# An adapter chain and a mixture of low-rank experts on one core: the helper products and the load order of the prologue rewritten

## The chip, the cores and the metric

The kernel runs on 1 core of one Trainium2 chip. Times are microseconds (us) of one execution on the device. The engines are TensorE (PE), VectorE (DVE), ScalarE (ACT), GpSimd (POOL) and SyncE (SP); SP and ACT issue the DMA transfers.

## The reference

x is 8 samples of 512 tokens with 2048 features, in float32. Two residual layers follow each other. The first adds a rank-16 adapter that is picked per sample; the second adds a dense product with W and two gated experts of rank 16 out of eight.

```
Bx = einsum('bni,bri->bnr', x, B0[adapter_ids]);  x = x + einsum('bnr,bor->bno', Bx, A0[adapter_ids])
base   = einsum('btd,od->bto', x, W)                       # W: 2048 x 2048
logits = einsum('btd,ed->bte', x, Wr) + 5 * one_hot(language_ids)[:, None]
gates  = softmax of the two largest logits, at their places, 0 elsewhere
h      = einsum('btd,erd->bter', x, A)
x      = x + base + 2 * einsum('bter,bte,eor->bto', h, gates, B)
```

## The kernel before

**Numbers.** Every float32 factor is split into a high part in fp32r (ScalarE casts it) and a low part (VectorE subtracts), and a product is made of three matmuls: high by high, low by high, high by low.

**Stages.** The first sample is handled apart, in 36 slots; each slot takes one 128-row strip of one quarter of W's columns, transposes it on PE (`w_transpose`, L637), copies it back (`w_keep`, ACT), forms four sums of it for the later samples (`w_sums`, DVE), writes these to DRAM (`w_store`, `w_sums_store`, SP), splits it (`pair_hi`, ACT; `pair_lo`, DVE) and multiplies (`first_products`, 24 matmuls of 512 columns). The other seven samples reread the prepared strips from DRAM.

**The prologue**, in `pe_start`, `act_start`, `dve_start`, `pool_start` and `sp_start` (L1081 to L1251), is what the change rewrites. It makes, for sample 0:

- `awb`, the helper columns: 16 blocks of 128 features, each with the 128 columns of the expert matrices A (`an`), the 8 router columns Wr (`wrn`) and the 16 adapter columns B0 of the current sample, as high and low part. A and Wr are transposed two blocks at a time into banks 0 and 1 of PSUM (`small_transpose`, L920), eight times in turn; the B0 rows of all eight samples (`b0n`) are transposed in four groups (`b0_transpose`, L942), and the columns of sample 0 are copied out of them.
- x of sample 0, transposed: 16 units u of two blocks by 256 tokens. A load m brings two units. A unit is transposed (`x_transpose`), copied out of PSUM by ACT (`x_keep`, L318), split into `xah` and `xal` (two places each, so unit u waits for the products of unit u-2), and multiplied with `awb` (`aux_products`, L351; 8 matmuls). Units 0 to 7 and 8 to 15 are two halves, both summed in banks 4 and 5, so the second half waits until the first has been copied out (`aux_low`, `aux_sum`).
- `a0t`, the adapter's output matrices A0 of all samples, reordered by POOL (`a0p`), transposed twice (`a0_transpose`, eight groups) and split, by rows (`a0_rows_hi`, `a0_rows_lo`) and by blocks; `g_products` (L1018, 32 matmuls) multiplies them with `awb`.
- The adapter itself: `bx_transpose`, `delta` (PE), `adapt` (DVE), then `first_hi` and `first_lo` split the new x for the slots.

**Order.** Each engine runs its own list as written; semaphores join them. In `pe_start` all helper columns come before the units of x; then twelve steps s each transpose unit 4+s, multiply unit s and transpose one group of A0. SP's list before the slots is: helper matrices, B0 rows, A0, the store of the split B0 (`b0_scr`), W strips 0 and 1, then, once both halves of `a0_rows_lo` are there (semaphore c_ar): three rows of `a0g`, the two stores of `a_scr`, W strip 2, the stores of strip 0, W strip 3, the stores of strip 1, and Bm (`bn`, placed in `ost`). ACT issues the eight loads of x. POOL reorders `bn` into `bnj` (placed in `xst`), and PE transposes `bnj` at the start of slot 1 (`bt_transpose(0)`, L1042):

```
for i in range(SLOTS0):            # pe_main
    ...
    if i in (1, 2):
        bt_transpose(e, 2 * i - 2)
```

Two more waits are used below. `w_keep(2, 0)` waits until the store of strip 0 has landed (semaphore d_bs0), because strip 2 goes into the same place; and PE transposes the second half of strip 2 only after that copy.

Of the kernel before, what the change touches and what calls it, by code (L numbers as in the profile page):

```python
# [5 lines left out]
def adapted_moe_lora_kernel(nc, x, adapter_ids, language_ids, A0, B0, W, Wr, A, Bm, out):  # L6
# [4 lines left out]
    P = 128  # L11
# [8 lines left out]
    AW = NAUX + R  # L20
    LOW = 256
# [67 lines left out]
    with ctx:  # L89
# [86 lines left out]
        def four(b, q, half):  # L176
# [3 lines left out]
        c_pool, c_lang, c_ap, c_aph, c_apl, c_bp, c_bph, c_bpl, c_bb = (  # L180
            sem(n) for n in ("c_pool", "c_lang", "c_ap", "c_aph", "c_apl", "c_bp", "c_bph", "c_bpl", "c_bb"))
# [3 lines left out]
        d_ids, d_lid, d_a, d_b0, d_a0, d_bn = (sem(n) for n in ("d_ids", "d_lid", "d_a", "d_b0", "d_a0", "d_bn"))  # L185
# [8 lines left out]
        d_u3 = [sem(f"d_u3{c}") for c in range(2)]  # L194
        c_tr, c_xc, c_xh, c_xl, c_ax = (sem(n) for n in ("c_tr", "c_xc", "c_xh", "c_xl", "c_ax"))
# [95 lines left out]

        def x_transpose(e, n, u):
# [24 lines left out]

        def x_keep(e, n, u):  # L318
            q, kp = x_unit(u)
            if kp == 0 and n >= 1:  # L320
                b = n - 1
                if n == 1:
                    e.wait_ge(c_l0, 16)
                elif q < 2:
                    if n == 2:
                        wait_used(e, SLOTS0 - 1)
                    else:
                        e.wait_ge(c_spl, split_of(b - 1, 6, 3) + 1)
                else:
                    e.wait_ge(c_spl, split_of(b, q, 3) + 1)  # L330
                    e.wait_ge(c_add, 8 * b)
            e.wait_ge(c_tr, 16 * n + u + 1)
            e.copy(two(n, q, kp), pb[:, x_bank(n, u), :]).then_inc(c_xc, 1)

        def x_hi(e, n, u):
# [6 lines left out]
            e.copy(xah[:, u % 2, :, :].rearrange("p k t -> p (k t)"), two(n, q, kp)).then_inc(c_xh, 1)  # L342

        def x_lo(e, n, u):
            q, kp = x_unit(u)
            e.wait_ge(c_xh, 16 * n + u + 1)
            e.tensor_tensor(out=xal[:, u % 2, :, :].rearrange("p k t -> p (k t)"), in0=two(n, q, kp),  # L347
                            in1=xah[:, u % 2, :, :].rearrange("p k t -> p (k t)").bitcast(f32), op=ALU.subtract)\
             .then_inc(c_xl, 1)

        def aux_products(e, n, u):  # L351
            q, kp = x_unit(u)
            if u % 8 == 0:
                if n == 0 and u == 0:
                    e.wait_ge(c_bb, 2)
                elif n and u == 0:
                    e.wait_ge(c_gd, GD * (n - 1) + 5)
                    e.wait_ge(d_bc, 16 * n)
                else:
                    e.wait_ge(c_gd, GD * n + 1)  # L360
            e.wait_ge(c_xl, 16 * n + u + 1)
# [1207 lines left out]
```

## Time and profile before

| | us |
|---|---|
| three timed runs | 1622.21, 1624.8, 1625.4 (median 1624.8) |
| the profiled execution | 1623.4 |
| its span, first to last instruction | 1621.6 |
| its first product with W starts at | 76.96 |
| its slot 1 starts at | 85.67 |

In the rows further down, the idle time in brackets is that of the engine just ahead of the instruction, with what ended it. The span's first 77 us are the prologue; from there PE is almost always busy, and a stage is read from the stretch it lies in, not from the whole.

### The profile page before, as it was taken

How to read it: one execution, taken by the hardware profiler on the slowest of the kernel's cores; microseconds unless marked ns; L12 is line 12 of the kernel's file. 1: busy time of each engine (PE TensorE's matmuls, PEld its weight loads, DVE VectorE, ACT ScalarE, POOL GpSimd, SP SyncE). 2: the span in 40 equal slices, each digit the busy share in tenths (PEclk: the TensorE clock that was granted, in tenths of full speed). 3: DMA queues.
4: the chain of work that ended last, by engine and by line, in shares of the span. 5: the costliest groups of instructions: out<-in, count | busy, mean ns of one | idle time of the engine just before them, and what ended most of it. 6: DMA issues, size and time to landing. Idle time of an engine off the chain costs nothing.

```text
span 1621.6 us, 21156 instructions
## 1 busy us (share of the span) xinstructions
PE 1587.1 (98%) x7744; PEld 1336.5 (82%) x7744; DVE 1176.2 (73%) x1599; ACT 758.7 (47%) x1000; POOL 9.8 (1%) x19
## 2 busy tenths in 40 slices
PE   7799999999999999999999999999999999999998
PEld 5687888788888888888888888888888888888887
DVE  3575444687778976888768876888769877787665
ACT  4553344344544554455444554445544544445443
POOL 1000000000000000000000000000000000000000
PEclk9899999999999999999999999999999999999999
DMA  8689797879886887879977797878877788576665
GB/s 240 190 214 252 211 241 188 214 220 239 204 220 220 220 218 197 233 224 230 219 200 230 217 232 191 234 223 224 214 200 233 222 227 205 195 234 207 207 217 161
DMA packets 396985, 351.30 MB, mean 217 GB/s; under 512 B 250522, under 2 KB 323530, under 8 KB 395850
## 3 DMA queue, kind: packets, MB, share of 16 engines
q1 hardware_dynamic: 394706, 345.76, 77.5%
q10 hardware_dynamic: 2176, 4.19, 0.9%
q8 instruction: 61, 1.00, 0.3%
q14 instruction: 42, 0.34, 0.1%
HBM read 280.62 MB, written 68.82 MB: 215 GB/s over the span
## 4 chain that ended last, share of the span: by engine, by line
PE 93%; DMA 2%; ACT 1%; SPq 1%; DVE 1%; issue 1%; ACTq 0%; DVEq 0%
PE pb L746 27%; PE pb L747 27%; PE pb L748 27%; PE pb L366 4%; PE pb L368 3%; PE pb L514 2%; PE pb L649 1%; SPq L625 1%; PE pb L314 1%; DMA raw<-in_L_cond_W_dram 1%; DMA wrn<-in_L_cond_Wr_dram 1%; ACT xah L342 0%; DMA t_scr<-raw 0%; DMA t_scr<-tst 0%; DMA bt_scr<-bt 0%
## 5 line engine op out<-in xcount | busy, mean ns | idle before, releaser
L742 DVE TENSOR_TENSOR wl<-raw,wh 128x1024 fp32r<-128x1024 f32 (+1 forms) x456 | 555.1, 1217 | 333.9 <-ACT wh L738 333.7
L738 ACT CAST wh<-raw 128x1024 fp32r<-128x1024 f32 (+1 forms) x456 | 477.1, 1046 | 683.7 <-PE pb L748 675.6
L746 PE MATMUL pb<-wh,sh 128*128 128x512 f32 x1568 | 612.8, 391 | 0.5 <-DVE ost L782 0.5
L747 PE MATMUL pb<-wl,sh 128*128 128x512 f32 x1568 | 611.6, 390 | 0.0
L748 PE MATMUL pb<-wh,sl 128*128 128x512 f32 x1568 | 611.2, 390 | 0.0
L748 PEld LDWEIGHTS pb<-wh,sl 128*128 128x128 f32 x1568 | 294.3, 188 | 62.8
L746 PEld LDWEIGHTS pb<-wh,sh 128*128 128x128 f32 x1568 | 294.6, 188 | 56.2 <-DVE wl L742 0.9
L747 PEld LDWEIGHTS pb<-wl,sh 128*128 128x128 f32 x1568 | 294.6, 188 | 55.0
L366 PE MATMUL pb<-awb,xah 128*128 128x304 f32 x512 | 138.4, 304 | 2.9 <-DVE aux L381 1.6
L368 PE MATMUL pb<-awb,xal 128*128 128x256 f32 x512 | 134.4, 280 | 0.0
L746 PE MATMUL pb<-wh,xh 128*128 128x512 f32 x256 | 106.2, 415 | 1.2 <-DVE ost L782 0.8
L366 PEld LDWEIGHTS pb<-awb,xah 128*128 128x128 f32 x512 | 96.1, 188 | 7.7 <-DVE aux L381 1.8
L748 PE MATMUL pb<-wh,xl 128*128 128x512 f32 x256 | 102.0, 399 | 0.0
L747 PE MATMUL pb<-wl,xh 128*128 128x512 f32 x256 | 101.9, 398 | 0.0
L368 PEld LDWEIGHTS pb<-awb,xal 128*128 128x128 f32 x512 | 96.3, 188 | 4.2
L588 DVE TENSOR_TENSOR sl<-pool_a,sh 128x512 fp32r<-128x512 f32 x120 | 82.0, 684 | 0.0
L347 DVE TENSOR_TENSOR xal<-pool_a,xah 128x512 fp32r<-128x512 f32 x88 | 60.3, 686 | 18.8 <-ACT xah L342 18.7
L583 ACT CAST sh<-pool_a 128x512 fp32r<-128x512 f32 x120 | 73.5, 613 | 0.0
L660 ACT COPY raw<-pb 128x512 f32<-128x512 f32 x64 | 37.7, 589 | 68.2 <-PE pb L649 58.9
L521 DVE TENSOR_TENSOR pool_a<-pool_a,pb 128x512 f32<-128x512 f32 x88 | 58.8, 680 | 11.9 <-PE pb L514 11.9
L342 ACT CAST xah<-pool_a 128x512 fp32r<-128x512 f32 x88 | 54.7, 623 | 25.2 <-DVE pool_a L262 13.8
L748 PEld LDWEIGHTS pb<-wh,xl 128*128 128x128 f32 x256 | 49.0, 192 | 10.9
(135 smaller groups left out, 1280.6 us busy)
## 6 DMA issues: line engine op xcount, KB each, us to landing
raw<-t_scr SPq DMA_DIRECT2D x392, 512.0 KB, 4.4
xst<-in_x_dram SPq DMA_DIRECT2D x768, 32.0 KB, 3.7
raw<-in_L_cond_W_dram SPq DMA_DIRECT2D x128, 128.0 KB, 3.9
t_scr<-tst SPq DMA_DIRECT2D x32, 512.0 KB, 5.1
raw<-bt_scr SPq DMA_DIRECT2D x28, 512.0 KB, 3.9
out_dram<-ost SPq DMA_DIRECT2D x28, 512.0 KB, 4.4
out_dram<-u SPq DMA_DIRECT2D x28, 512.0 KB, 3.4
t_scr<-raw SPq DMA_DIRECT2D x32, 256.0 KB, 4.1
```

The source lines that it names most:

```text
L342: e.copy(xah[:, u % 2, :, :].rearrange("p k t -> p (k t)"), two(n, q, kp)).then_inc(c_xh, 1)
L347: e.tensor_tensor(out=xal[:, u % 2, :, :].rearrange("p k t -> p (k t)"), in0=two(n, q, kp), in1=xah[:, u % 2, :, :].rearrange("p k t -> p ...
L366: e.matmul(pb[:, 4 + t, 0:2 * AW], xah[:, u % 2, k, toks], cols[:, 0:2 * AW], start=u % 8 == 0 and k == 0, stop=False)
L368: last = e.matmul(pb[:, 4 + t, 0:LOW], xal[:, u % 2, k, toks], cols[:, 0:LOW], start=False, stop=u % 8 == 7 and k == 1)
L521: e.tensor_tensor(out=two(n, q, kp), in0=two(n, q, kp), in1=pb[:, delta_bank(n, u), :], op=ALU.add)\
L583: e.copy(sh[:, h % SR, :, :].rearrange("p k t -> p (k t)"), two(b, SUM_QUARTER[product], kp)).then_inc(c_sph, 1)
L588: e.tensor_tensor(out=sl[:, h % SR, :, :].rearrange("p k t -> p (k t)"), in0=two(b, SUM_QUARTER[product], kp), in1=sh[:, h % SR, :, :].rea ...
L738: e.copy(pair_split(wh, g), pair_source(g)).then_inc(c_wh, 1)
L742: e.tensor_tensor(out=pair_split(wl, g), in0=pair_source(g), in1=pair_split(wh, g).bitcast(f32), op=ALU.subtract).then_inc(c_wl, 1)
L746: e.matmul(o, h, wh[:, g % RING, k, :], start=start, stop=False)
L747: e.matmul(o, h, wl[:, g % RING, k, :], start=False, stop=False)
L748: return e.matmul(o, l, wh[:, g % RING, k, :], start=False, stop=stop)
```

## The change

- A is transposed in four groups of four blocks (`a_transpose`), each filling one of the banks 0 to 3; Wr and the B0 rows of sample 0 alone, loaded into rows 8 to 23 of `wrn`, are transposed as 16 pieces of 24 columns into bank 5 (`small_transpose`). Five copies and five subtractions take the place of eight and eight, and of the two copies of B0 columns.
- The transposes of all eight samples' B0 move from before the first units to steps 3 to 6, those of A0 from steps 3 to 10 to steps 7 to 14; the 32 `g_products` move behind step 15, in three parts between the steps of the adapter.
- Odd units of x are copied out of PSUM by DVE (`x_keep_dve`), even ones by ACT. `xah0` and `xal0` give two more places, so unit u waits for the products of unit u-4. The second half of the sums goes to banks 2 and 3.
- 18 transposes of `ident` (`warm`) stand ahead of everything on PE.
- SP issues seven of the eight loads of x, ahead of and between B0, A0 and W; W strips 0 and 1 are issued ahead of the store of B0.
- In the slots, `w_transpose(2, 1)` moves into slot 0, (3, 1) to the start of slot 1, and so on for the first two slots, and `first_hi` waits piece by piece for the memory that it overwrites. The split places share memory with the prologue's, so five of these are put in another order.

PE, from the first transposes to the first helper product. Before (`an`, `wrn`, `b0n` are A, Wr and B0 as loaded, `xst` and `ost` hold x):

```order
L314 MATMUL pb<-ident,xst 128x128 [waits d_x00,c_pool]
...
L927 MATMUL pb<-ident,an 128x128 [waits d_a]
L928 MATMUL pb<-ident,wrn 128x8
...
L927 MATMUL pb<-ident,an 128x128 [waits c_apl]
...
L948 MATMUL pb<-ident,b0n 128x128 [waits d_b0]
L948 MATMUL pb<-ident,b0n 128x128 x7
L948 MATMUL pb<-ident,b0n 128x128 [waits c_bpl]
...
L314 MATMUL pb<-ident,xst 128x128 [waits c_xc,d_x01]
...
L366 MATMUL pb<-awb,xah 128x304 [waits c_xl,c_bb]
```

And after:

```order
L957 MATMUL pb<-ident 128x128 [waits c_pool]
L957 MATMUL pb<-ident 128x128 x17
L321 MATMUL pb<-ident,xst 128x128 [waits d_x00]
...
L963 MATMUL pb<-ident,an 128x128 [waits d_a]
L963 MATMUL pb<-ident,an 128x128 x7
L969 MATMUL pb<-ident,wrn 128x24 [waits d_wr]
L969 MATMUL pb<-ident,wrn 128x24 x15
L963 MATMUL pb<-ident,an 128x128 x8
L321 MATMUL pb<-ident,xst 128x128 [waits c_x00,d_x01]
...
L388 MATMUL pb<-awb,xah 128x304 [waits c_xl,c_apl]
```

The waits of the transposes on the subtractions (c_apl) and the B0 transposes are gone from this place.

SP, from A0 to the stores that follow it. Before:

```order
L1223 DMA a0n<-in_L_cond_A_dram 128x256 [waits c_tr]
L1223 DMA a0n<-in_L_cond_A_dram 128x256 x7
L1227 DMA b_scr<-b0h 2048x1x128 [waits c_bpl]
L1227 DMA b_scr<-b0l 2048x1x128
L625 DMA raw<-in_L_cond_W_dram 128x2x128 [waits c_tr]
L625 DMA raw<-in_L_cond_W_dram 128x2x128 x7
L1234 DMA a0g<-a0n 16x2048 [waits c_pool,c_ar]
```

And after:

```order
L283 DMA xst<-in_x_dram 128x2x512 [waits c_tr]
L1281 DMA a0n<-in_L_cond_A_dram 128x256 x8
L283 DMA ost<-in_x_dram 128x2x512 [waits c_tr] x2
L658 DMA raw<-in_L_cond_W_dram 128x2x128 x8
L1289 DMA b_scr<-b0h 2048x1x128 [waits c_bpl]
L1289 DMA b_scr<-b0l 2048x1x128
L1293 DMA a0g<-a0n 16x2048 [waits c_pool,c_ar]
```

The last loads of x stand between the others, and the W strips stand ahead of the store of B0. From the row of `a0g` on, SP's list is the same up to Bm in both.

PE, between the adapter and slot 0. Before (`st` holds the adapter's inner product, `raw` a W strip, L514 is `delta`):

```order
L649 MATMUL pb<-ident,raw 128x128 [waits c_wc,d_raw0]
...
L398 MATMUL pb<-ident,st 128x128 [waits c_xc,c_gd]
...
L649 MATMUL pb<-ident,raw 128x128 [waits c_wc]
...
L514 MATMUL pb<-bxt,a0g 128x256 [waits d_ar,c_ga]
...
L746 MATMUL pb<-wh,xh 128x512 [waits c_l0,c_wl]
```

And after:

```order
L542 MATMUL pb<-bxt,a0g 128x256 [waits d_ar,c_ga]
...
L682 MATMUL pb<-ident,raw 128x128 [waits c_wc]
...
L542 MATMUL pb<-bxt,a0g 128x256 [waits c_x1]
...
L682 MATMUL pb<-ident,raw 128x128 [waits c_wc,d_raw0]
L682 MATMUL pb<-ident,raw 128x128 x3
L682 MATMUL pb<-ident,raw 128x128 [waits c_wc]
L682 MATMUL pb<-ident,raw 128x128 x3
L779 MATMUL pb<-wh,xh 128x512 [waits c_l0,c_wl]
```

The adapter now stands ahead of strip 2's transposes instead of behind them.

The core of the diff:

```diff
 def x_hi(e, n, u):
-    e.wait_ge(c_xc, 16 * n + u + 1)
-    if 16 * n + u >= 2:
+    wait_kept(e, n, u)
+    if n:
         e.wait_ge(c_ax, 16 * n + u - 1)
+    elif u >= 4:
+        e.wait_ge(c_ax, u - 3)
...
+def aux_bank(n, half):
+    return 2 if n == 0 and half else 4
...
+def warm(e):
+    e.wait_ge(c_pool, 3)
+    for m in range(18):
+        e.transpose(pb[:, 4, m % 4 * P:(m % 4 + 1) * P], ident[:, :], ident[:, :])
+
+def a_transpose(e, m):
+    if m == 0:
+        e.wait_ge(d_a, 16)
+    for k in range(4):
+        last = e.transpose(pb[:, m, k * P:(k + 1) * P], an[:, (4 * m + k) * P:(4 * m + k + 1) * P], ident[:, :])
+    last.then_inc(c_ap, 1)
+
+def small_transpose(e):
+    e.wait_ge(d_wr, 32)
+    for k in range(KT):
+        last = e.transpose(pb[:, 5, k * ES:(k + 1) * ES], wrn[0:ES, k * P:(k + 1) * P], ident[0:ES, 0:ES])
+    last.then_inc(c_ap, 1)
...
 def pe_start(e):
+    warm(e)
     for u in range(2):
         x_transpose(e, 0, u)
-    for m in range(8):
-        small_transpose(e, m)
-    for m in range(4):
-        b0_transpose(e, m)
+    for m in range(2):
+        a_transpose(e, m)
+    small_transpose(e)
+    for m in range(2, 4):
+        a_transpose(e, m)
     for u in range(2, 4):
         x_transpose(e, 0, u)
-    for s in range(12):
-        x_transpose(e, 0, 4 + s)
+    for s in range(16):
+        if s < 12:
+            x_transpose(e, 0, 4 + s)
         aux_products(e, 0, s)
-        if s >= 3:
-            a0_transpose(e, s - 3) if s < 11 else g_products(e)
-    for s in range(12, 16):
-        w_transpose(e, (s - 12) // 2, s % 2)
-        aux_products(e, 0, s)
+        if 3 <= s < 7:
+            b0_transpose(e, s - 3)
+        if 7 <= s < 15:
+            a0_transpose(e, s - 7)
+        if 12 <= s < 15:
+            w_transpose(e, (s - 12) // 2, (s - 12) % 2)
+    g_products(e, range(8))
+    bx_transpose(e, 0)
+    g_products(e, range(8, 12))
+    for u in range(2):
+        delta(e, 0, u)
+    g_products(e, range(12, 16))
+    w_transpose(e, 1, 1)
+    for u in range(2, 4):
+        delta(e, 0, u)
     w_transpose(e, 2, 0)
-    bx_transpose(e, 0)
-    w_transpose(e, 2, 1)
-    for u in range(4):
-        delta(e, 0, u)
...
 def dve_start(e):                      # steps 10 to 12, in the new order
+        if s in (11, 12):
+            a0_rows_lo(e, s - 11)
+        if 11 <= s < 15:
+            a0_lo(e, s - 11)
+        if s in (10, 12):
+            add_identity(e, (s - 10) // 2)
...
 def sp_start(e):
+    e.dma_start(wrn[E:ES, :], B0[bass.ds(adapter[0], 1), :, :].rearrange("a r d -> (a r) d")).then_inc(d_wr, 16)
+    for m in range(1, 5):
+        x_load(e, 0, m)
     ...                                # lid and the eight loads of b0n
+    x_load(e, 0, 5)
     ...                                # the eight loads of a0n
+    for m in range(6, 8):
+        x_load(e, 0, m)
+    for g in range(2):
+        first_load(e, g)
     e.wait_ge(c_bpl, 4)
     ...                                # the stores of b0h and b0l
-    e.wait_ge(c_tr, 10)
-    for g in range(2):
-        first_load(e, g)
     e.wait_ge(c_ar, 2)
```

## Rows read from the trace of the kernel before

**Rows 1.** The page: shares of the chain that ended last

```profile
PE 93%; DMA 2%; ACT 1%; SPq 1%; DVE 1%; issue 1%; ACTq 0%; DVEq 0%
```

**Rows 2.** Windows: stretch, length, busy by engine, PEclk, DMA share, GB/s

```profile
10.30:29.30 19.00, 15.99 (x60) 10.87 (x60) 7.99 (x15) 10.42 (x21) 1.89 (x1) 1.00 0.82 207
45.00:54.00 9.00, 8.47 (x66) 8.24 (x67) 6.55 (x10) 6.99 (x12) 0.00 (x0) 1.00 0.01 3
54.00:79.00 25.00, 17.81 (x101) 15.55 (x100) 12.63 (x26) 11.30 (x21) 0.09 (x1) 0.78 0.97 259
75.00:80.00 5.00, 4.58 (x14) 3.61 (x14) 4.92 (x10) 2.88 (x5) 1.09 (x2) 0.50 1.05 328
124.80:1621.00 1496.20, 1485.79 (x7176) 1250.57 (x7176) 1106.73 (x1466) 695.31 (x892) 0.00 (x0) 1.00 0.79 217
```

**Rows 3.** Timeline of PE up to the first helper product: start, length, instruction [idle]

```profile
10.34 0.48 PE L927 MATMUL pb<-ident,an 128*128 128x128 f32 x1 [2.88 <-DMA wrn<-in_L_cond_Wr_dram]
13.91 0.48 PE L927 MATMUL pb<-ident,an 128*128 128x128 f32 x1 [1.07 <-DVE awb L938]
23.71 1.97 PE L948 MATMUL pb<-ident,b0n 128*128 128x128 f32 x8 [0.55 <-DVE b0l L959]
25.47 1.85 PE L314 MATMUL pb<-ident,xst 128*128 128x128 f32 x8
29.33 0.38 PE L366 MATMUL pb<-awb,xah 128*128 128x304 f32 x1 [1.34 <-DVE xal L347]
```

**Rows 4.** Timeline of PE: starts of steps without (two) and with A0

```profile
30.43 0.60 PE L314 MATMUL pb<-ident,ost 128*128 128x128 f32 x4
31.91 0.60 PE L314 MATMUL pb<-ident,ost 128*128 128x128 f32 x4
37.19 0.60 PE L314 MATMUL pb<-ident,xst 128*128 128x128 f32 x4
39.09 0.60 PE L314 MATMUL pb<-ident,xst 128*128 128x128 f32 x4
```

**Rows 5.** Windows of the transfers alone, columns as in Rows 2

```profile
2.10:26.10 24.00, 16.08 (x59) 11.13 (x60) 5.45 (x11) 7.39 (x15) 1.94 (x3) 1.00 0.96 241
30.00:42.00 12.00, 12.00 (x102) 12.00 (x101) 4.98 (x9) 10.22 (x17) 0.00 (x0) 1.00 1.06 322
```

**Rows 6.** Timeline of POOL: the A0 reorder and the Bm reorder

```profile
26.07 1.89 POOL L1205 COPY a0p<-a0n 128x2048 f32<-128x2048 f32 x1 [22.06 <-DMA a0n<-in_L_cond_A_dram]
78.91 4.66 POOL L1208 COPY xst<-ost 128x256 f32<-128x256 f32 x8 [50.94 <-DMA ost<-in_L_cond_B_dram]
```

**Rows 7.** Timeline of DVE: a subtraction of 512 columns, and one of A0's rows

```profile
51.80 0.68 DVE L1003 TENSOR_TENSOR a0l<-pb,a0h 128x512 fp32r<-128x512 f32 x1
52.63 1.22 DVE L1015 TENSOR_TENSOR a0p<-a0t,a0n 128x1024 fp32r<-128x1024 f32 x1
```

**Rows 8.** Timeline of SP's DMA issues behind c_ar

```profile
53.88 1.25 SPq L1234 DMA_DIRECT2D a0g<-a0n  x2
57.10 1.28 SPq L1236 DMA_DIRECT2D a_scr<-a0p  x1
60.66 3.84 SPq L625 DMA_DIRECT2D raw<-in_L_cond_W_dram  x4
65.06 0.47 SPq L684 DMA_DIRECT2D t_scr<-raw  x1
66.69 0.36 SPq L689 DMA_DIRECT2D t_scr<-tst  x1
```

**Rows 9.** Timeline of ACT: the copy of strip 2's first half

```profile
71.33 0.58 ACT L660 COPY raw<-pb 128x512 f32<-128x512 f32 x1 [2.42 <-DMA t_scr<-raw]
```

**Rows 10.** Timeline of PE: strip 2, the first product with W, slot 1's first transposes

```profile
71.97 1.11 PE L649 MATMUL pb<-ident,raw 128*128 128x128 f32 x4 [1.44 <-ACT raw L660]
76.96 0.77 PE L746 MATMUL pb<-wh,xh 128*128 128x512 f32 x1 [0.42 <-DVE xl L536]
85.67 0.60 PE L1049 MATMUL pb<-ident,xst 128*128 128x128 f32 x4
```

More of the change, by code:

```diff
@@ L194, in adapted_moe_lora_kernel @@
         d_u3 = [sem(f"d_u3{c}") for c in range(2)]
+        c_x0 = [sem(f"c_x0{n}") for n in range(2)]
         c_tr, c_xc, c_xh, c_xl, c_ax = (sem(n) for n in ("c_tr", "c_xc", "c_xh", "c_xl", "c_ax"))
@@ L1123, in act_start @@
-            x_load(e, 0, 5)
+            x_keep_act(e, 0)
             for u in range(2):
                 x_hi(e, 0, u)
-            for s in range(12):
-                x_keep(e, 0, 4 + s)
-                if s in (1, 3):
-                    x_load(e, 0, (11 + s) // 2)
+            for m in range(2):
+                a_hi(e, m)
+            small_hi(e)
+            for m in range(2, 4):
+                a_hi(e, m)
+            x_keep_act(e, 2)
+            x_hi(e, 0, 2)
+            for s in range(15):
+                if s < 12 and s % 2 == 0:
+                    x_keep_act(e, 4 + s)
@@ L1142, in act_start @@
-            w_keep(e, 0, 1)
+                    a0_copy(e, s - 7)
+                if s in (11, 12):
+                    a0_rows_hi(e, s - 11)
+                if 11 <= s < 15:
+                    a0_hi(e, s - 11)
+                if s in (12, 13):
+                    w_keep(e, 0, s - 12)
             pair_hi(e, 0)
+            aux_low(e, 0, 1)
+            bx_hi(e, 0)
             w_keep(e, 1, 0)
+            bx_keep(e, 0)
+            for u in range(2):
+                first_hi(e, u)
             g_low(e)
@@ L1163, in dve_start @@
             for u in range(2):
                 x_lo(e, 0, u)
-            bias_columns(e)
-            for s in range(12):
+            for m in range(2):
+                a_lo(e, m)
+            small_lo(e)
+            for m in range(2, 4):
+                a_lo(e, m)
+            x_keep_dve(e, 3)
+            x_lo(e, 0, 2)
+            for s in range(15):
+                if s < 12 and s % 2:
+                    x_keep_dve(e, 4 + s)
                 if s == 8:
                     aux_sum(e, 0, 0)
-                x_lo(e, 0, s + 2)
-                if 7 <= s < 11:
-                    a0_lo(e, s - 7)
-                if s in (8, 10):
-                    a0_rows_lo(e, (s - 8) // 2)
-                if s == 11:
-                    add_identity(e, 0)
-                    add_identity(e, 1)
@@ L1193, in dve_start @@
+            g_sum(e)
+            for u in range(2, 4):
+                adapt(e, 0, u)
+            for u in range(2, 4):
+                first_lo(e, u)
+            g_lo(e)
+            pair_lo(e, 1)
+            w_sums(e, 1)
+            add_identity(e, 2)
             add_identity(e, 3)
```

263 lines of the change are left out of this document (128 added, 135 removed).

## The prediction

> **What bounds the kernel now.** I read the chain of waits first, by shares: PE carries 93% of the path that ended last [rows 1]. Then the windows. From slot 6 on (124.8 us) PE is busy for 1485.79 of 1496.20 us [rows 2]; the change removes no matmul there, so nothing is to be had behind the first slots. What can move is the moment at which the slots begin: the first product with W starts at 76.96 and slot 1 at 85.67 [rows 10]. I therefore forecast by how much slot 1 starts earlier, and take the rest as it is.
>
> Three stretches of the prologue wait for different things. Up to 29.33 PE has too little ready: it waits 2.88 for A and Wr, then runs transposes in turn with copies [rows 3]. From there the steps run at 1.48 us each without a group of A0 (30.43 to 31.91) and 1.90 with one (37.19 to 39.09) [rows 4]. From 54 to 79 the DMA engines are busy at a share of 0.97, after 9 us at 0.01 [rows 2]: everything behind the semaphore c_ar (both halves of `a0_rows_lo` done) is one queue of transfers. Two of these hold PE. The copy of strip 2's first half waits 2.42 for the store of strip 0 and starts at 71.33 [rows 9], with the second transposes of that strip behind it at 71.97 [rows 10]; and POOL can reorder Bm only from 78.91, until 83.57 [rows 6], ahead of slot 1's first transposes at 85.67, 2.1 us of slack.
>
> I call A the time of c_ar: 53.88 now, when SP issues `a0g` [rows 8].
>
> **The change, part by part.**
>
> *To the first helper product.* The transposes of Wr and B0, the eight turns with their waits (1.07 in the first [rows 3]) and the 16 transposes of B0 leave this place. Left behind the load at 10.34 are 16 transposes of A, 16 narrow ones, and three units of x of four each: 44. Eight transposes took 1.97 at 23.71 [rows 3], with the drain of the last in it; I take 0.22 each, also for the narrow ones, whose price the trace lacks (not above that of a wide one; below, at least nothing). That is 9.7 us at this rate, so 20.0. These are durations of the 1.2 GHz level, although the granted-clock column says 1.00 in that window [rows 2]. At 2.4 GHz it is half, 4.9, and 15.2, plus the last copies and subtractions (PE's idle time there was 1.34 [rows 3]): 16.5. Half of A may be done before the B0 rows are in. I take **17.5**, nearer to the fast end because PE then works without stops, against 29.33.
>
> Of the clock, the Trainium skill (TensorE: Matmul & The Clock Gate, Part 1) says that half rate is the default and that activity lifts it. The 1.97 us above agree; whether 18 dummy transposes ahead of a wait for A lift it for good, no row of before can show, so this sum rests on no gain from them. They cost nothing either: 18 x 0.22 is 4 us, and PE has no other work before 10.34 but two units of x.
>
> *The steps.* Steps 0 to 2 carry no group, 3 to 6 one of B0, 7 to 10 one of A0: 3 x 1.48 + 8 x 1.90 = 19.6, so step 11 begins at 37.1. The stop between the halves goes with the second pair of banks. DVE takes over half of the copies. A copy of 512 columns out of PSUM by DVE is not in the trace; a subtraction of that size is 0.68 [rows 7], ACT's copy 0.58 [rows 9]; I take 0.68. In two steps with B0 DVE then has two subtractions of x, two of B0 and one copy, 3.4 us against 3.8 on PE: hidden. If it were not, each such pair would cost the excess.
>
> *To A.* In steps 11 and 12 DVE has the copy of unit 15, two subtractions of x, one of A0's blocks (4 x 0.68) and both row halves (2 x 1.22 [rows 7]): 5.2, less some overlap, behind the transpose of unit 15 (0.4): A = 37.1 + 5.4 = **42.5**.
>
> *Do the transfers keep up?* By the shapes, ahead of the end of A0 now stand six loads of x (0.52 MB each), A, B0 and A0 (1.05 each) and 0.2 of Wr and B0: 6.5 MB. At 241 GB/s, the rate of 2.1 to 26.1 [rows 5], they end at 29.1. POOL's reorder adds 1.89 [rows 6]: 31.0. It is needed at the end of step 7, 17.5 + 4 x 1.48 + 4 x 1.90 = 31.0: just in time, with nothing to spare. The last two loads of x and strips 0 and 1 (2.1 MB) at 322 GB/s [rows 5] end at 35.6; strip 0 is in by 34, and DVE's `add_identity` wants it in step 10, at about 36. The store of split B0, another 2.1 MB, ends at 42.1, just ahead of A. SP's waits for transposes of x (loads 4 to 7) are met in time on these numbers, but A0 and W stand behind them on SP.
>
> *From A to slot 1.* SP's list behind A is the same. Before, Bm was reordered 83.57 - 53.88 = 29.7 after A. In that stretch SP itself stood twice: from 58.38 to 60.66 for the transposes of strip 0, and about 1.2 ahead of 66.69 for its sums [rows 8]. Both will now be done in time, so without them it is 26.2. That gain is real only if SP and not the DMA engines set the pace; these were busy at 0.97 [rows 2], so I stay near the upper end: 28.5, and Bm is ready at **71.0**. The other path: the store of strip 0 landed 71.33 - 53.88 = 17.5 after A, or 15.2 without SP's first wait; the copy (0.58) and the second transposes (0.5 to 1.1) follow, so the first product starts 16.3 to 19.1 after A, at 58.8 to 61.6 instead of 76.96. The adapter, which took 72 to 77 before, now lies under that wait. Slot 0 took 8.7, some of it at a clock of 0.50 [rows 2]; if nothing changes there, slot 1 could start at 67.5 to 70.3. Bm comes later than that, so part of what PE wins is handed back at `bt_transpose(0)`.
>
> *Sum.* Slot 1 starts at 71.0 instead of 85.67: 14.7 earlier. What follows (the load that PE waits for at 121.6, the wait for strips) hangs on the slots and moves with them; W strips 5 and 6 are released up to half a slot later, but SP reaches them no earlier anyway. The profiled execution took 1623.4 (median of three 1624.8): 1623.4 - 14.7 = **1608.7**. A between 40 and 47 and 26.2 to 29.7 behind it give 66 to 77 for slot 1, so 1604 to 1614.5 for this case alone.
>
> **Rivals.**
>
> *The transfers become the bound.* For it: everything above is just in time, and between 10.3 and 29.3 they ran at only 207 GB/s [rows 2]. If all 10.2 MB up to the store of B0 run at 207, they end at 51.4, and `a0g` stands behind them: 51.4 + 28.5 = 79.9 for slot 1, 5.8 earlier, 1617.6. Against it: the narrow B0 loads and late issues weigh on that rate, and 241 and 322 were measured around it. The Trainium skill (DMA: Bandwidth & Descriptors, Issuing engines are not separate DMA queues) says that all issuing engines' transfers share the same 16 DMA engines; by that rule moving x from ACT's to SP's list changes the order and no rate, which leaves this rival open.
>
> *Faster still.* The clock rises early (first helper product at 16.5 or less), A comes at 40, the path behind it takes 26.2, and the 3 us that PE waits at 121.6 shrink as well: 1623.4 - 19.5 - 3 = 1601.
>
> *Slower than before: PE stays at 1.2 GHz through the steps.* The granted clock was 0.50 from 75 to 80, after PE had stood several times [rows 2]. If the new steps stop PE as often (A0, strip 0, loads of x just in time), each step takes twice its time: 39.2 instead of 19.6, from 20 to 59; A = 65, slot 1 at 93, 8 us later than now: 1631. It turns from gain to loss when A passes 85.67 - 28.5 = 57.2, that is when some 60% of the steps' work runs at half rate. Against it: the steps before kept the full rate, at 1.48 and 1.90, in spite of their stops. The rule of the page named above would allow it only where PE stands.
>
> **How the numbers follow.** Forecast 0.72, transfers 0.14, faster still 0.08, low clock 0.06 (half of it within 0.2%, half beyond). A measurement of this kernel can tell about 0.2%, 3.2 us, from no change. So faster 0.94, same 0.03, slower 0.03. The range takes the forecast's own 1604 to 1614.5 and reaches a little to both neighbours: 1602 to 1616.
>
> **What would show it.** In the new profile: the first aux product near 17.5; steps of 1.5 and 1.9 with no wait for A0 at step 7; `a0g` issued near 42.5; the first product with W near 60; a wait of 1 to 4 us at slot 1's first transposes, ended by POOL; slot 1 at 71. It is wrong if PE waits in the steps for transfers, if the steps take 3 us, or if what is won by slot 1 is lost again before slot 8.

## The result, and the profile after

| | us |
|---|---|
| before, four timed runs | 1622.21 to 1625.4, median 1623.95 |
| after, four timed runs | 1610.85 to 1611.55, median 1610.89 |
| after : before | 0.9921, 95% interval 0.9904 to 0.9938 |
| profiled execution before, after | 1623.4, 1611.55 |
| their spans | 1621.6, 1609.8 |

The kernel became 13 us faster by the medians and 11.85 us by the two profiled executions; the forecast was 14.7 from the profiled one, to 1608.7, with a range of 1602 to 1616.

PE's timeline up to the first helper product answers [rows 3] (start, length, instruction, in brackets the idle time ahead and what ended it):

```profile
1.62 4.10 PE L957 MATMUL pb<-ident 128*128 128x128 f32 x18 [1.62 <-POOL ident L1253]
...
9.25 1.10 PE L963 MATMUL pb<-ident,an 128*128 128x128 f32 x8 [1.94 <-DMA an<-in_L_cond_A_dram]
10.53 1.89 PE L969 MATMUL pb<-ident,wrn 24*128 24x24 f32 x16 [0.17 <-DMA wrn<-in_L_cond_B_dram]
12.35 1.97 PE L963 MATMUL pb<-ident,an 128*128 128x128 f32 x8
...
16.68 0.60 PE L388 MATMUL pb<-awb,xah 128*128 128x304 f32 x1
...
23.03 0.66 PE L999 MATMUL pb<-ident,b0n 128*128 128x128 f32 x4 [0.39 <-DMA b0n<-in_L_cond_B_dram]
```

The first helper product (L388; its start is called t0 from here on) comes at 16.68 instead of 29.33. From there to 42 the timeline has only one wait of PE, 0.39 for B0 at 23.03. The narrow transposes cost 1.89 / 16 = 0.12 each.

Most of what t0 won was not idle time. In the kernel before, A's transposes and the narrow ones of Wr ran in turn, and the timeline shows no idle time between 13.91 [rows 3] and 21.19:

```profile
14.32 0.27 PE L928 MATMUL pb<-ident,wrn 8*128 8x8 f32 x1
14.52 0.47 PE L927 MATMUL pb<-ident,an 128*128 128x128 f32 x1
```

A pair took 14.52 - 13.91 = 0.61. The 16 pairs took 10.85 (10.34 to 21.19, one wait of 1.07 among them). The same 16 of A and 16 wider ones, sorted by kind, take 4.86 now (9.25 to 14.11), and 5.49 (9.79 to 15.28) in the run without dummies further down, where none of them is at the higher rate. The 16 transposes of all samples' B0, another 4.28 (21.19 to 25.47), have left this place. These two make 10.3 of the 12.65 us. This is read from rows; no run here puts the alternation or the B0 transposes back.

SP's timeline answers [rows 8], POOL's [rows 6]. SP's first:

```profile
22.10 8.71 SPq L658 DMA_DIRECT2D raw<-in_L_cond_W_dram  x8
43.17 1.25 SPq L1293 DMA_DIRECT2D a0g<-a0n  x2
47.71 5.99 SPq L658 DMA_DIRECT2D raw<-in_L_cond_W_dram  x4
59.41 0.49 SPq L1301 DMA_DIRECT2D ost<-in_L_cond_B_dram  x1
```

And POOL's:

```profile
28.41 1.90 POOL L1259 COPY a0p<-a0n 128x2048 f32<-128x2048 f32 x1 [24.39 <-DMA a0n<-in_L_cond_A_dram]
67.41 4.10 POOL L1262 COPY xst<-ost 128x256 f32<-128x256 f32 x8 [37.10 <-DMA ost<-in_L_cond_B_dram]
```

A, the issue of `a0g`, is at 43.17 instead of 53.88; Bm is issued at 59.41 and reordered until 71.51.

PE's timeline from strip 2 on answers [rows 10]. `raw` at L682 is a half of a W strip; (2,1) is the second half of strip 2. Shown are (2,0), (2,1), the first product, the start of slot 1 (L1094), then (4,1) and (5,0), and two later halves on which a reading further down rests:

```profile
57.22 1.11 PE L682 MATMUL pb<-ident,raw 128*128 128x128 f32 x4 [4.34 <-DMA raw<-in_L_cond_W_dram]
60.70 1.12 PE L682 MATMUL pb<-ident,raw 128*128 128x128 f32 x4 [2.36 <-ACT raw L693]
61.47 0.78 PE L779 MATMUL pb<-wh,xh 128*128 128x512 f32 x1
...
71.56 0.65 PE L1094 MATMUL pb<-ident,xst 128*128 128x128 f32 x4 [1.74 <-POOL xst L1262]
...
79.37 0.60 PE L682 MATMUL pb<-ident,raw 128*128 128x128 f32 x4
80.73 0.63 PE L682 MATMUL pb<-ident,raw 128*128 128x128 f32 x4 [0.33 <-ACT raw L693]
...
281.98 0.66 PE L682 MATMUL pb<-ident,raw 128*128 128x128 f32 x4 [2.87 <-DMA raw<-in_L_cond_W_dram]
291.02 0.63 PE L682 MATMUL pb<-ident,raw 128*128 128x128 f32 x4 [1.95 <-issue]
```

Slot 1 starts at 71.56 behind POOL's reorder of Bm, 14.1 us earlier than before. But the end of the span is only 11.8 earlier: 2.3 us are lost behind slot 1. The windows (stretch, length, busy by engine, granted clock, DMA share, GB/s) answer [rows 2]:

```profile
38.00:41.00 3.00, 3.00 (x27) 2.99 (x27) 2.94 (x6) 3.00 (x6) 0.00 (x0) 1.00 0.78 215
41.00:43.20 2.20, 2.00 (x18) 1.77 (x17) 2.20 (x4) 1.97 (x4) 0.00 (x0) 1.00 0.01 3
...
43.00:60.00 17.00, 10.94 (x78) 9.93 (x76) 12.41 (x24) 8.17 (x16) 0.00 (x0) 0.85 0.94 238
60.00:72.00 12.00, 9.55 (x40) 7.73 (x41) 7.33 (x13) 4.02 (x6) 4.10 (x8) 0.79 0.95 291
```

The 9 us of idle DMA engines ahead of A have shrunk to two, and behind A they are as full as before.

**Five points.** I read the same five points from every trace: t0, A, T (the start of the transposes of strip half (5,0), slot 2), X (the transposes of the last unit of the second sample's x, in slot 24), and D (the last `delta` of the second sample, in slot 34). The columns are the stretches between them in us; slot 1 lies between A and T.

| trace | t0 | t0 to A | A to slot 1 | A to T | T to X | X to D | D to end |
|---|---|---|---|---|---|---|---|
| before | 29.33 | 24.55 | 31.79 | 39.97 | 164.61 | 73.66 | 1289.48 |
| after | 16.68 | 26.49 | 28.39 | 37.56 | 164.73 | 74.88 | 1289.46 |
| the 12 experiments | 16.46 to 23.53 | 25.54 to 33.88 | 23.52 to 28.87 | 34.62 to 43.59 | 164.01 to 167.29 | 73.58 to 76.21 | 1289.40 to 1289.49 |

Between the profiles of before and after the end moved by -12.65 + 1.94 - 2.41 + 0.12 + 1.22 - 0.02 = -11.8. Eight of the experiments (all of the second group below) have the helper columns and the steps of after unchanged; over them and the kernel after itself t0 spreads from 16.46 to 17.84 and t0 to A from 25.5 to 26.5. About a microsecond in these columns is therefore not told from chance.

### The profile page after: what moved, and what is told of

Read it like the earlier page. It is cut to its first block, busy times and chain, and to the rows that moved or that the text cites. A ratio compares the mean times of both kernels' runs of the same rounds, so it can differ in the third digit from the quotient of the medians.

```text
span 1609.8 us, 21189 instructions
## 1 busy us (share of the span) xinstructions
PE 1580.3 (98%) x7762; PEld 1334.6 (83%) x7762; DVE 1180.3 (73%) x1603; ACT 754.5 (47%) x988; POOL 9.3 (1%) x19
## 4 chain that ended last, share of the span: by engine, by line
PE 92%; issue 3%; DMA 2%; SPq 1%; DVE 1%; POOL 0%; ACT 0%; POOLq 0%; ACTq 0%; DVEq 0%
PE pb L779 27%; PE pb L780 27%; PE pb L781 27%; PE pb L388 4%; PE pb L390 3%; PE pb L542 2%; PE pb L682 1%; DMA t_scr<-tst 1%; DMA a0n<-in_L_cond_A_dram 1%; PE pb L321 0%; DMA bt_scr<-bt 0%; SPq L658 0%; DMA raw<-in_L_cond_W_dram 0%; PE pb L957 0%; POOL xst L1262 0%
## 5 line engine op out<-in xcount | busy, mean ns | idle before, releaser
L388 PE MATMUL pb<-awb,xah 128*128 128x304 f32 x512 | 138.7, 304 | 0.0
L388 PEld LDWEIGHTS pb<-awb,xah 128*128 128x128 f32 x512 | 96.4, 188 | 4.4
L781 PEld LDWEIGHTS pb<-wh,xl 128*128 128x128 f32 x256 | 48.5, 189 | 10.7
```

Of the source, the lines that this page charges most:

```text
L388: e.matmul(pb[:, aux_bank(n, u // 8) + t, 0:2 * AW], x_high(n, u)[:, k, toks], cols[:, 0:2 * AW], start=u % 8 == 0 and k == 0, stop=False)
L781: return e.matmul(o, l, wh[:, g % RING, k, :], start=False, stop=stop)
```

## Experiments: the front of the prologue

Theory: the helper columns come early because PE, the loads and the places for split x all allow it, and nothing in the steps waits. Rival: one part alone does the work and the others are idle. Each run undoes one part. The regrouping of A and Wr and the move of B0's transposes are undone by none.

**The dummy transposes left out.**

```diff
 def pe_start(e):
-    warm(e)
+    e.wait_ge(c_pool, 3)
```

> The 18 dummy transposes at the start of PE's list (4.10 us from 1.62) are left out; PE waits for the identity instead. Theory: they run while PE has nothing else, and PE fell back to 1.2 GHz behind them anyway (eight transposes of A took 1.97 from 12.35): first helper product at 16.7 to 18, time +0 to +1.5, 1611 to 1612.4. Rival: they bring the clock up; without them transposes stay at 0.22 each up to the first product and some steps run at half rate: first product at 18 to 20, step 11 later by 3 us or more, 1614 or above.

Measured: 1610.96 us, ratio to before 0.9912 (0.9895 to 0.9928). PE's timeline:

```profile
9.79 1.97 PE L963 MATMUL pb<-ident,an 128*128 128x128 f32 x8 [2.32 <-DMA an<-in_L_cond_A_dram]
...
17.85 0.60 PE L388 MATMUL pb<-awb,xah 128*128 128x304 f32 x1
```

The first eight transposes of A take 1.97 here and 1.10 in the kernel after; the next eight take 1.97 in both. But of the twelve traces with the dummies only three have 1.09 or 1.10 for that group; three have 1.63 to 1.76 and six 1.93 to 1.97. So the dummies lift PE for one group at most, by up to 0.9 us, and in half of the traces not at all. t0 is 1.17 later, at the end of the spread of equal code, A 0.6, within it, and in the time nothing is left. The rival was right on the transposes, which all stay at the low rate, and falls on the steps: from 18.8 on the products take 0.31 to 0.30 without any dummy.

**x loaded by ACT.** The four first loads of x stand at the head of ACT's list, the others among its copies; SP issues none. The expectation calls these ACT's old places, which is not exact: in the kernel before, ACT waited for A and Wr ahead of its second load, and here it doesn't.

```diff
 def act_start(e):
-    x_load(e, 0, 0)
+    for m in range(4):
+        x_load(e, 0, m)
...
 def sp_start(e):
-    for m in range(1, 5):
-        x_load(e, 0, m)
...
-    x_load(e, 0, 5)
...
-    for m in range(6, 8):
-        x_load(e, 0, m)
```

> All loads of x are issued by ACT again, at ACT's old places among its copies; SP's list is the rest. Theory: the order in which transfers are issued sets when A, B0 and A0 are in; with six loads of x no longer ahead of them they come sooner, and x later or not: first product 0 to 2 us earlier, x loads 5 to 7 late behind ACT's copies; time within 1.5 us of 1610.9 in either direction. Rival: it was the move of the loads that brought the first product from 29.33 to 16.68 and step 11 to 36.88: then step 11 comes 3 to 6 us later and the time is 1614 to 1617.

Measured: 1618.42 us, 0.9958 (0.9941 to 0.9975). PE's timeline, and then the line on the loads of the tile `ost` up to 30 us:

```profile
10.33 1.97 PE L963 MATMUL pb<-ident,an 128*128 128x128 f32 x8 [3.13 <-DMA an<-in_L_cond_A_dram]
...
22.76 1.12 PE L321 MATMUL pb<-ident,ost 128*128 128x128 f32 x4 [5.34 <-DMA ost<-in_x_dram]
23.53 0.60 PE L388 MATMUL pb<-awb,xah 128*128 128x304 f32 x1
```

```profile
DMA to landing us min/median/max: 6.5/21.0/22.5
```

Two of the loads, issued at 1.7 and 2.2, need 21.0 and 22.5 us, while SP's B0, A0 and W are in flight beside them; in the kernel after such a load needs 9.1 (median of its tile). The rate was lower too: from 10 to 24 the DMA engines moved 197 GB/s here and 264 in the kernel after. What share of the delay belongs to the order and what to the rate, no run separates. PE stands 5.34 us, t0 is 23.53, A 50.94, and everything behind follows: 7.8 us in A, 7.5 in the time. The theory that the order does little falls; the rival holds in its direction, and its size was too small. With this order of loads 6.85 of the 12.65 us gained at t0 would be gone.

**Two places for split x.**

```diff
 def x_high(n, u):
-    return (xah0 if n == 0 and u % 4 >= 2 else xah)[:, u % 2, :, :]
+    return xah[:, u % 2, :, :]
...                                    # x_low in the same way
 def x_hi(e, n, u):
-    elif u >= 4:
-        e.wait_ge(c_ax, u - 3)
+    elif u >= 2:
+        e.wait_ge(c_ax, u - 1)
```

> Split x again has two places instead of four; all else stays. Theory: with two places the split of a unit waits for the product of two units before, so DVE's subtractions come one step late: 0.2 to 0.5 us per step, A 2 to 5 us later, slot 1 by as much, 1612.5 to 1616. Rival: the subtractions are made in time with two places also, since steps are bound by PE: within 0.5 us, 1611.

Measured: 1619.5 us, 0.9965 (0.9952 to 0.9979). t0 is 17.35, but A is 51.23, 8.06 later. PE's timeline in the steps, and DVE's:

```profile
35.10 0.41 PE L388 MATMUL pb<-awb,xah 128*128 128x304 f32 x1 [1.23 <-DVE b0l L1010]
44.29 0.63 PE L1031 MATMUL pb<-ident,a0t 128*128 128x128 f32 x4 [1.79 <-ACT a0t L1036]
49.52 0.65 PE L1031 MATMUL pb<-ident,a0t 128*128 128x128 f32 x4 [1.67 <-DVE a0l L1045]
```

```profile
46.69 0.69 DVE L363 TENSOR_TENSOR xal<-pool_a,xah 128x512 fp32r<-128x512 f32 x1 [1.75 <-ACT xah L358]
```

ACT's split waits for a place and DVE's subtraction for ACT. The subtractions and copies of B0 and A0 stand behind these two on the lists of DVE and ACT, so PE waits for those. The direction was the theory's, the size (2 to 5) too small: each late split holds up what is queued behind it.

**All copies of x on ACT.** In the lists of ACT and DVE the odd units' copies change sides:

```diff
-    if s < 12 and s % 2 == 0:
-        x_keep_act(e, 4 + s)
+    if s < 12:
+        (x_keep_dve if s % 2 else x_keep_act)(e, 4 + s)      # both now on ACT
...                                    # units 1 and 3, and DVE's list, in the same way
```

> ACT makes all copies of x out of PSUM, DVE none (as in the kernel before). Theory of the prediction: in a step with A0 PE's 1.90 covers either split of the copies; ACT's load per step is about 2.0 then: step 11 later by 0 to 1 us, time +0 to +1, 1611 to 1612. Rival: the copies are what sets the steps; with ACT alone each step of two units takes 0.3 to 0.5 more, step 11 some 3 us later, 1614.

Measured: 1613.4 us (1610.74 to 1614.56), 0.9923 (0.9907 to 0.994), not told from the kernel after. PE's timeline has the steps with groups of B0 and A0 at 1.90 each; the starts of steps 4 and 11:

```profile
24.30 0.60 PE L321 MATMUL pb<-ident,xst 128*128 128x128 f32 x4
...
37.61 0.60 PE L321 MATMUL pb<-ident,ost 128*128 128x128 f32 x4
```

(37.61 - 24.30) / 7 = 1.90, as with DVE's help: PE hides either split, and the rival falls. t0 to A is 27.02, half a microsecond above the spread.

## Experiments: behind A

The prediction had the rest "move with the slots". Since 14.1 us at slot 1 gave 11.8 at the end, the question is what sets the time behind A: the start of slot 1, the bytes in the queue of transfers, or something else.

**The old places of three strip halves.** (3,1), (4,0) and (4,1) and their copies go back to where the kernel before had them.

```diff
 def pe_main(e):
-    if i < 2:
+    if i == 0:
         w_transpose(e, i + 2, 1)
...
-    if i < 2:
+    if i == 0:
         w_transpose(e, i + 3, 0)
...
-    if i >= 2 and more:
+    if more:
         w_transpose(e, i + 3, 1)
...
-    if i == 1:
-        w_transpose(e, 4, 1)
```

> The transposes of three halves of strips (second half of strip 3, both of strip 4) and their copies go back to the places in slots 0 and 1 that they had in the kernel before. Theory: their new places cost what was given back between slot 1 (14.1 us earlier than before) and slot 2 (13.05 earlier): PE waits 0.33 at 80.73 for ACT's copy and runs 0.44 of transposes more there. Then slot 2 comes 0.5 to 0.9 us earlier and the time is 1610.0 to 1610.4. Rival: slot 1 is bound by Bm, and the same transposes stand ahead of it or behind it: less than 0.2 us, or worse where a copy is waited for.

Measured: 1610.9 us, 0.9912 (0.9899 to 0.9925), no difference. PE's timeline, slot 1 and (5,0):

```profile
71.15 0.66 PE L1094 MATMUL pb<-ident,xst 128*128 128x128 f32 x4 [0.95 <-POOL xst L1262]
...
79.41 0.60 PE L682 MATMUL pb<-ident,raw 128*128 128x128 f32 x4
```

Slot 1 to T is 8.26 us here, 8.18 before and 9.17 after: the 0.9 was read rightly. But T to X takes 165.06 and X to D 75.09, and from A to the end this trace has 1566.55 against 1566.63. The 0.9 is not there at the end; the stretches that differ behind T differ by less than their spread over the runs.

**The stores of split A behind Bm's load.**

```diff
 def sp_start(e):
-    for s, t in enumerate((arh, arl)):
-        e.dma_start(a_scr[s, :, 0:D], t).then_inc(d_as, 16)
     first_load(e, 2)
...
     e.dma_start(bn, Bm.rearrange("e (p j) r -> p e j r", p=P)).then_inc(d_bn, 16)
+    for s, t in enumerate((arh, arl)):
+        e.dma_start(a_scr[s, :, 0:D], t).then_inc(d_as, 16)
```

> The two stores of split A rows (1.05 MB each, issued 45.10 and 46.39 in the changed kernel) go behind the load of Bm in SP's list; nothing else moves. Theory: between A (43.17) and slot 1 the transfers are one queue that sets the pace (share 1.00 to 1.08 from 50 to 70). Then 2.1 MB less stand ahead of the stores of strip 0 and of Bm: first product with W at 55 to 57 instead of 61.47, Bm ready 5 to 6 us earlier, slot 1 at 65 to 67 instead of 71.56, and the time 3 to 6 us below the changed kernel's 1610.9, about 1606. Rival: SP's issue and the waits of PE and ACT set the pace; then slot 1 stays within 1 us of 71.56 and the time is unchanged.

Measured: 1612.28 us (1610.19 to 1615.43), 0.992 (0.9907 to 0.9933), no difference. PE's timeline: slot 1, (5,0), (5,1):

```profile
66.09 0.66 PE L1094 MATMUL pb<-ident,xst 128*128 128x128 f32 x4 [0.33 <-POOL xst L1262]
...
78.66 1.11 PE L682 MATMUL pb<-ident,raw 128*128 128x128 f32 x4 [3.73 <-DMA raw<-in_L_cond_W_dram]
84.39 0.60 PE L682 MATMUL pb<-ident,raw 128*128 128x128 f32 x4
```

The stage came as the theory said: first product at 57.00, slot 1 at 66.09. The time did not. PE, 5.5 us early at slot 1, stands 3.73 us for strip 5, which SP issued 30.54 us behind A, and 30.80 in the kernel after. Behind that stop the transposes take 1.11 instead of 0.60 for a while, and (5,1) comes 5.73 behind (5,0) instead of 4.17. This is the run that decides: an earlier slot 1 is worth nothing while strip 5 is issued no earlier.

**Both together.** The two diffs above.

> Both edits: split A stored behind Bm's load, and the three halves of strips transposed in their old places. If both gains are real and independent: 1605 to 1606. If the pace is set elsewhere: 1610 to 1611. If only the stores count: as with them alone, about 1606.

Measured: 1610.21 us, 0.9904 (0.989 to 0.9919). Slot 1 is at 67.49, PE stands 2.16 at (4,0), T is at 79.71. Neither gain reaches the end.

**Bm loaded ahead of A.**

```diff
 def sp_start(e):
+    e.wait_ge(c_tr, 16)
+    e.dma_start(bn, Bm.rearrange("e (p j) r -> p e j r", p=P)).then_inc(d_bn, 16)
     e.wait_ge(c_ar, 2)
...
-    e.dma_start(bn, Bm.rearrange("e (p j) r -> p e j r", p=P)).then_inc(d_bn, 16)
```

> The load of Bm (1.05 MB) goes ahead of SP's wait for A, into the stretch from 38 to 43 where the DMA engines fall to a share of 0.01 (41.0 to 43.2); all else stays. Two theories for what sets slot 6 and all behind it. Transfers: from A to about 132 the DMA engines are one full queue, and the end is A plus the bytes in it. Then 1.05 MB less at 238 to 290 GB/s bring the stretch from 111 on 3.6 to 4.4 us forward, and the time to 1606.5 to 1607.5. Start of the slots: it goes by when slot 1 starts. Bm no longer holds it, slot 1 comes 1.5 to 3 us earlier, and the time is 1608 to 1609.5. If neither holds, 1610 to 1611.5.

Measured: 1609.46 us (1608.67 to 1610.74), 0.991 (0.9896 to 0.9923). SP's issue of strip 5, and the window of the transfers:

```profile
74.57 2.65 SPq L658 DMA_DIRECT2D raw<-in_L_cond_W_dram  x4
```

```profile
60.00:72.00 12.00, 10.42 (x45) 8.78 (x46) 6.42 (x13) 4.02 (x6) 0.00 (x0) 0.71 0.73 214
```

The theory of transfers falls: the DMA engines now have a gap (0.73 from 60 to 72, where after had 0.95), and the time is above its range. The other is not settled by this run: Bm no longer holds slot 1, which comes 1.39 us earlier behind A, T (80.13) as much, and the median lies at the upper end of its range. Strip 5 is issued 30.59 us behind A, and 30.80 in the kernel after.

**With the old places too.** That diff and the one of the strip halves.

> The early load of Bm together with the old places of the three halves of strips. By the theory of transfers the places add nothing that lasts, 1606.5 to 1607.5 as with the load alone; if PE's order in slots 0 and 1 counts once Bm is out of the way, 0.5 to 1 us less than with the load alone.

Measured: 1610.34 us (1606.96 to 1611.21), 0.9909 (0.9895 to 0.9924): nothing more, T 36.12 behind A as against 36.15.

**The stores of split B0 behind Bm's load.**

```diff
 def sp_start(e):
-    e.wait_ge(c_bpl, 4)
-    for s, t in enumerate((b0h, b0l)):
-        e.dma_start(b0_scr[:, :, s, :], t[:, :, :]).then_inc(d_b0s, 16)
...
     e.dma_start(bn, Bm.rearrange("e (p j) r -> p e j r", p=P)).then_inc(d_bn, 16)
+    e.wait_ge(c_bpl, 4)
+    for s, t in enumerate((b0h, b0l)):
+        e.dma_start(b0_scr[:, :, s, :], t[:, :, :]).then_inc(d_b0s, 16)
```

> The opposite: the two stores of split B0 (2.1 MB), which run ahead of A at 31 to 41, go behind the load of Bm, into the full stretch. Slot 1 does not depend on them. Transfers: 2.1 MB more at 238 to 290 GB/s, the stretch from 111 on is 7 to 9 us later, slot 1 less than 1 us, and the time is 1617 to 1620. Start of the slots: slot 1 within 1 us of 71.56, and the time 1610 to 1612.

Measured: 1619.44 us, 0.9973 (0.9963 to 0.9982). SP's issue of strip 5, and PE at slot 1 and at T:

```profile
81.94 2.66 SPq L658 DMA_DIRECT2D raw<-in_L_cond_W_dram  x4
```

```profile
71.73 0.66 PE L1094 MATMUL pb<-ident,xst 128*128 128x128 f32 x4 [0.59 <-POOL xst L1262]
87.44 1.11 PE L682 MATMUL pb<-ident,raw 128*128 128x128 f32 x4 [5.21 <-DMA raw<-in_L_cond_W_dram]
```

Slot 1 is where it was (71.73), and the time is 8.5 us worse. Strip 5 is issued 38.09 behind A, 7.3 later than after; 2.1 MB in 7.3 us is 288 GB/s, about the 291 of the full window of after. PE stands 5.21 for it. From the other side this says what the stores of split A said: strip 5 counts, and slot 1 alone does not.

**All three moves, in two orders.** Bm early, the old places, and the stores of split A behind the load of strip 4, or just ahead of it:

```diff
 def sp_start(e):                      # first order; the second has the two stores one line up
-    for s, t in enumerate((arh, arl)):
-        e.dma_start(a_scr[s, :, 0:D], t).then_inc(d_as, 16)
...
     w_store(e, 1)
     first_load(e, 4)
+    for s, t in enumerate((arh, arl)):
+        e.dma_start(a_scr[s, :, 0:D], t).then_inc(d_as, 16)
```

> Bm loaded early, the three halves of strips in their old places, and the two stores of split A behind the load of strip 4. Two theories. Chain: behind A not the sum of bytes counts but what stands ahead of the next strip that PE wants; with Bm and split A both out of the way of strips 2, 3 and 4, the first product comes at about 55, slot 1 at 63 to 65, no strip is waited for by more than 2 us before slot 5, and the transposes of the last unit of the next rows of x (245.46 in the changed kernel, 202.3 behind A) come 4 to 6 us earlier behind A; time 1605 to 1607. Bytes: the queue to 132 holds the same bytes behind A as with Bm alone moved, so as there (200.1 to 201.0 behind A), 1609 to 1610.

> The same, but the two stores of split A ahead of the load of strip 4 instead of behind it. Chain: strip 4 is late again, as with the stores behind Bm's load, where PE waited 3.73 for it at 78.66: 2 to 4 us of the gain are lost, time 1608 to 1610. Bytes: the same as the run before, 1609 to 1610.

Measured: 1611.96 us (1609.24 to 1612.41), 0.9919 (0.9905 to 0.9932) for the first, and 1607.82 (1607.29 to 1607.94), 0.9898 (0.9883 to 0.9914) for the second: the other way round. SP's list in the first order (strip 4, the first store of split A, strip 5), and PE at T:

```profile
58.24 1.91 SPq L658 DMA_DIRECT2D raw<-in_L_cond_W_dram  x4
60.19 1.51 SPq L1303 DMA_DIRECT2D a_scr<-a0n  x1
...
74.11 2.64 SPq L658 DMA_DIRECT2D raw<-in_L_cond_W_dram  x4
```

```profile
79.70 1.12 PE L682 MATMUL pb<-ident,raw 128*128 128x128 f32 x4 [2.87 <-DMA raw<-in_L_cond_W_dram]
```

And in the second (first store, strip 4, strip 5):

```profile
55.16 0.49 SPq L1302 DMA_DIRECT2D a_scr<-a0n  x1
...
57.51 4.65 SPq L658 DMA_DIRECT2D raw<-in_L_cond_W_dram  x4
...
71.80 2.60 SPq L658 DMA_DIRECT2D raw<-in_L_cond_W_dram  x4
```

```profile
77.38 0.66 PE L682 MATMUL pb<-ident,raw 128*128 128x128 f32 x4 [2.75 <-DMA raw<-in_L_cond_W_dram]
```

I had looked at strip 4 alone. Ahead of strip 4 the two stores use the time in which SP waits for strip 2's transposes anyway; behind it they stand ahead of strip 5, which is issued 31.09 behind A in the first order and 29.04 in the second. T follows at 36.68 and 34.62. The second order has the earliest T behind A of all, and each of its four runs is below each of the four of the kernel after, by about 3 us at the medians. The two intervals still overlap, and 1.6 us of the 4.1 between the two orders arise only between X and D, so I call it probably the best version, by 2 to 3 us.

**What strip 5 waits for.** The lists of SP and DVE answer this in all 14 traces. On SP's list the load of strip 5 stands directly behind the store of strip 2's sums (`w_sums_store`), and it is issued within 0.05 us of that store's end. The store begins when DVE has made the sums, and in eleven traces DVE had waited with them until the store of strip 1's sums had landed, since both use the tile `tst`. In the run with the stores of split A behind Bm's load, DVE's first sum of strip 2, and SP:

```profile
70.29 0.42 DVE L702 TENSOR_TENSOR tst<-raw 128x256 f32<-128x256 f32 x1 [4.52 <-DMA t_scr<-tst]
```

```profile
71.88 0.97 SPq L722 DMA_DIRECT2D t_scr<-tst  x1
72.89 2.60 SPq L658 DMA_DIRECT2D raw<-in_L_cond_W_dram  x4
```

DVE, like PE, came early and stood 4.52 for that store. The load also needs the place of strip 3, which is free once (3,1) is transposed, but that seldom holds it: in the runs with the old places, alone and with Bm early, (3,1) was done by 67.45 and 67.60, and strip 5 was issued at 73.46 and 73.53. T follows that issue by 5.50 to 5.95 us in the eight runs of this group, wherever slot 1 lies, and by 5.72 in the kernel before. In the kernel after it is 6.76; there strip 5 was in 1.1 us before PE came to it. In the last two runs the store of strip 1's sums was issued at 62.2 both times; it landed at 70.21 where the stores of split A had been issued just ahead of it, and at 67.31 in the other order.

## Why the prediction was right, and where its steps were off

**Right: what moves and where.** The prediction let the prologue's start set everything up to A and slot 1, and it did. t0 came at 16.68 (forecast 17.5), A at 43.17 (42.5), POOL's end of Bm 28.3 behind A (28.5), slot 1 28.4 behind A with a wait of 1.74 for POOL (1 to 4 forecast). First product 18.3 behind A, in the range of 16.3 to 19.1. A0 was in at 28.4, no step waited for it, and DVE's copy out of PSUM took 0.69 (priced 0.68).

**Mis-sized, cancelling in part.** The narrow transposes were priced at up to 0.22 and took 0.12, worth 1.6 us, half of the distance to the slow bound of 20.0. That the trace lacked their price is not exact: the narrow ones of Wr took 0.20 each there, in turn with A's, and what cost time in that place was the turn itself, 0.61 a pair, and not the waits on copies, of which there was one. The steps and what follows to A were short by 1.5 (42.5 - 17.5 = 25.0 against 26.49). Each lies near the spread of equal code; that the two cancel is luck.

**Off: "what follows hangs on the slots and moves with them".** This is the term that failed; it was set at nothing and cost 2.3 us. 0.99 of it lies between slot 1 and T: the moved transposes of (4,1) stand ahead of (5,0), whose PSUM bank ACT must first copy out (the wait of 0.33). I had listed this move and priced only its loads. 0.12 lies between T and X, and 1.22 between X and D. There PE stood 1.83 for a strip's load and 1.75 for nothing that the profile shows before, and 2.87 and 1.95 after (at 282 and 291). In the twelve experiments that stretch, the same code in each, takes 73.58 to 76.21. The five traces in which X comes latest, the one of before among them (249 to 258), lie at 73.58 to 73.92; of the nine others (243 to 246) eight lie at 74.44 to 76.21, and only the second of the last two orders, at 73.68, does not. So some of a gain is probably handed back there when the slots come early. No run tests this, and the cause is open.

**Right for a reason too narrow.** The sum ran through slot 1. Runs in which slot 1 came 4 to 5.5 us earlier (66.09, 67.49 and 67.42) and strip 5 was issued 30.5 to 31.1 behind A (30.80 in the kernel after) gained nothing, and the one that left slot 1 alone and made strip 5 late lost 8.5. What carries the prologue's gain to the end is A: where A came 8.06 and 7.77 later (two places, x loaded by ACT), the time was 8.6 and 7.5 longer. Behind A it is the chain of stores and sums on SP and DVE that ends in the load of strip 5. The change moved that load from 88.13 to 73.97, 14.2 earlier, as much as slot 1, and so the sum through slot 1 came out. Its remark that SP reaches strips 5 and 6 no earlier anyway named the right engine. No run shortened that chain alone.

**The rivals.** *Transfers become the bound* did not happen: from t0 to A PE waited for no load but B0's, 0.39. (Its 10.2 MB should be 10.7 by the prediction's own terms, which would have given 1620 instead of 1617.6.) *Faster still* came near at t0 (16.5 or less) and was wrong on all else. *PE stays at 1.2 GHz*: the eight transposes of A from 12.35 on still took 1.97, the rate of 1.2 GHz, but the products reached 0.30 within a microsecond of t0. The Trainium skill (TensorE: Matmul & The Clock Gate, Part 1) says that activity lifts the clock, and the run without dummies agrees: in unbroken work its products went from 0.60 at 17.85 to 0.31 at 18.77. On the order of loads, the Trainium skill says that DMAs of all issuing engines interleave on the same 16 DMA engines (DMA: Bandwidth & Descriptors, Issuing engines are not separate DMA queues). This fits too: the two loads that needed 21.0 and 22.5 us had been issued by ACT at 1.7 and 2.2, and six loads of B0 that SP issued from 3.9 on had landed by 20.7.

## What to carry to other kernels

Before counting a gain at the first main loop iteration, look two or three iterations on for the load that can't be issued earlier, and at what stands just ahead of it on its issuer's list: if that one stays, the gain is a wait. When an in-order engine serves several streams, one place more for the stream at its head can be worth more than its own wait, since all that is queued behind it moves. Repeat a stage's reading over several traces of equal code before explaining its last microsecond.

## What the runs showed of the hardware that I had not expected

- An early issue is no early landing: two loads of 512 KB issued at 1.7 and 2.2 us landed 21.0 and 22.5 us later, with later transfers of another engine beside them; where SP issued them in order among its own, 9.1.
- After a stop of 2.8 to 5.2 us at strip 5, the transposes took 1.11 for four instead of 0.60 to 0.66 in three of four traces, and in all four (5,1) followed 5.64 to 5.82 us behind (5,0) instead of 4.10 to 4.17. The granted clock was 0.60 from 78 to 81 in the run that stopped for 3.73, against 1.00 from 84 to 87. A stop in the slots cost about 1.6 us more than itself.
- The granted-clock column said 1.00 over 10 to 15 us in the run without dummies, where eight transposes took 1.97, twice their 1.10. Durations told the level there, the column did not. With the dummies the same eight took 1.10 behind a stop of 1.94, 1.97 behind one of 3.13 (x loaded by ACT) and 1.09 behind one of 3.31 (the first of the last two orders), so the length of the stop alone does not decide it.
